# Ten instead of eight head pairs' score maxima in the expert phase, as full-array matmuls over zero-padded keys

## The reference

```python
xn = _layernorm(x)
# attention: a second layer norm, 16 heads of 8 features, softmax over 1024 keys
zn = (xn - mu) / jnp.sqrt(var + 1e-05) * ln_w + ln_b
q, k, v = split_heads(zn @ W_qkv + b_qkv)
attn = jax.nn.softmax(jnp.einsum('bhqd,bhkd->bhqk', q, k) / sqrt(8), axis=-1)
s = xn + concat_heads(attn @ v) @ W_proj + b_proj
# experts: all 8 are computed, the best 2 by the router count
h = gelu(xn @ W1[e] + b1[e])            # 128 -> 512
expert_out = h @ W2[e] + b2[e]          # 512 -> 128
g = silu(sum_e weights[:, e] * expert_out[e])
out = x + s * g
```

## Time and profile before

| | us |
|---|---|
| time, median of 3 runs (1129.79 to 1131.89) | 1130.94 |
| profiled execution, its time | 1131.14 |
| its span | 1129.3 |

### The profile page before, as it was taken

The page is one execution under the profiler, slowest core; times in us unless marked ns, Lnnn a source line. Parts: engine busy times, 40 slices in busy tenths (PEclk is TensorE's granted clock), DMA queues, the critical chain, the costliest instruction groups (busy, mean ns, idle before and its releaser), DMA issues.

```text
span 1129.3 us, 17260 instructions
## 1 busy us (share of the span) xinstructions
PE 1062.4 (94%) x6041; PEld 438.8 (39%) x6041; DVE 896.3 (79%) x1567; ACT 847.7 (75%) x1133; POOL 365.0 (32%) x534
## 2 busy tenths in 40 slices
PE   5698999999999999999999999999999999999995
PEld 4475656566666666663122222222121212212123
DVE  7566778777768687666999999999999999999715
ACT  6575666566666666667988898888889898988982
POOL 3795656656666666453010001000000000000001
PEclk9899999999999999998999999999999999999998
DMA  4523131414141322223111112111211111111102
GB/s 144 150 83 84 61 86 29 117 34 118 32 114 33 102 51 64 75 72 92 45 44 44 39 35 56 32 45 29 58 31 44 40 48 45 30 44 30 30 1 75
DMA packets 84992, 67.42 MB, mean 60 GB/s; under 512 B 9277, under 2 KB 71402, under 8 KB 84906
## 3 DMA queue, kind: packets, MB, share of 16 engines
q1 hardware_dynamic: 84906, 66.32, 21.7%
HBM read 51.08 MB, written 15.20 MB: 59 GB/s over the span
## 4 chain that ended last, share of the span: by engine, by line
PE 53%; ACT 19%; DVE 6%; issue 4%; ACTq 0%; DVEq 0%; POOL 0%; POOLq 0%
ACT p_ring L753 17%; PE psum L947 13%; PE psum L927 11%; PE psum L867 6%; PE psum L832 4%; PE psum L848 3%; PE psum L834 3%; PE psum L833 3%; PE psum L856 2%; PE psum L853 2%; PE psum L854 2%; DVE neg_max_half L1237 2%; PE psum L960 2%; DVE neg_max_half L1219 1%; PE psum L981 1%
## 5 line engine op out<-in xcount | busy, mean ns | idle before, releaser
L753 ACT ACTIVATE p_ring<-psum 128x1024 f32<-128x1024 f32 x512 | 500.7, 1023 | 66.0 <-PE psum L927 62.3
L1219 DVE TENSOR_REDUCE neg_max_half<-psum 128x1 f32<-128x512 f32 x768 | 486.3, 684 | 38.1 <-PE psum L867 29.0
L867 PE MATMUL psum<-k_max_stack,q_max_stack 48*128 48x512 bf16 x1024 | 300.6, 386 | 15.7 <-DVE neg_max_half L1237 9.6
L927 PE MATMUL psum<-q_stack,k_stack 51*128 51x512 bf16 x1024 | 279.1, 383 | 12.9 <-ACT p_ring L753 3.7
L947 PE MATMUL psum<-p_ring,v_sb 128*9 128x512 f32 x2048 | 268.5, 597 | 0.4 <-ACT o_sb L744 0.4
L716 ACT ACTIVATE h_hi<-psum,cols 128x512 fp32r<-128x512 f32 x192 | 132.0, 688 | 152.1 <-PE psum L834 147.9
L612 POOL TENSOR_TENSOR h_lo<-h_split,h_hi 128x512 fp32r<-128x512 f32 x128 | 164.5, 1289 | 141.0 <-ACT h_split L719 139.2
L1237 DVE TENSOR_REDUCE neg_max_half<-psum 128x2 f32<-128x1024 f32 x128 | 156.5, 1222 | 60.6 <-PE psum L867 60.4
L927 PEld LDWEIGHTS psum<-q_stack,k_stack 51*128 51x128 bf16 x1024 | 60.3, 94 | 305.8 <-ACT p_ring L753 281.4
L568 POOL CAST neg_max_parts<-neg_max_rest 128x16 bf16<-128x16 f32 x32 | 6.7, 211 | 510.6 <-DVE neg_max_rest L1228 510.6
L719 ACT ACTIVATE h_split<-psum,cols 128x512 f32<-128x512 f32 x192 | 130.9, 682 | 0.0
(11 more groups left out here) (114 smaller groups left out, 920.4 us busy)
## 6 DMA issues: line engine op xcount, KB each, us to landing
expert_w_bc<-expert_w_dram SPq DMA_DIRECT2D x64, 256.0 KB, 4.9
k_rows_dram<-qk_parts SPq DMA_DIRECT2D x24, 256.0 KB, 3.0
q_max_stack<-q_rows_dram SPq DMA_DIRECT2D x64, 96.0 KB, 2.5
k_max_stack<-k_rows_dram SPq DMA_DIRECT2D x64, 96.0 KB, 2.5
q_stack<-q_rows_dram SPq DMA_DIRECT2D x64, 96.0 KB, 2.5
k_stack<-k_rows_dram SPq DMA_DIRECT2D x64, 96.0 KB, 2.5
q_rows_dram<-qk_parts SPq DMA_DIRECT2D x8, 384.0 KB, 2.6
xz<-in_L_attn_z_dram SPq DMA_DIRECT2D x8, 256.0 KB, 3.2
```

The source lines that it names most:

```text
L753: act.activation(p_sb[:, n % PR, a, :, :].rearrange("p h t -> p (h t)"), scores_bank[s % 2], ACT.Exp, scale=SCALE).then_inc(S("P"), 1)
L867: return pe.matmul(to, q_m[rows, slot, t * P:(t + 1) * P], k_m[rows, slot, c * TG:(c + 1) * TG], start=True, stop=True)
L927: i = pe.matmul(scores_bank[s % 2][:, hh * TG:(hh + 1) * TG], k_s[rows, slot, kt * P:(kt + 1) * P], q_s[rows, slot, a * TG:(a + 1) * TG], ...
L1219: dve.tensor_reduce(mx[:, p % MXR, c, hh * NT + t:hh * NT + t + 1], ring_bank(("max", u)), AX.X, ALU.max, negate=True).then_inc(S("R"), 1)
```

## The change

- The first ten head pairs, not eight, have their maxima in the expert phase: 160 early units, in slots HT + 4 + (27 m) // 20, again from slot 36 to 250. 704 singles are left, over the same 240 blocks.
- k_m gets a second copy of its rows, one for each head: k_m[:, slot, 0, :] holds head 0's rows and zeros elsewhere, k_m[:, slot, 1, :] head 1's. An early unit is two matmuls with all 128 rows of q_m (both heads) as stationary operand and one of these as moving operand. The singles of the attention phase still use their 48 rows. Zeros are written once, k_m by VectorE and q_m by POOL at the start; SP's first row loads wait for both.
- w_t has no tile of its own and lies in xnT; ScalarE's copy into xnT therefore waits for the store of the group before.
- EARLY_TURN has ten entries: slots 60, 90, 122, 126, 154, 186, 190, 218, 233, 254 (before: 66, 92, 122, 154, 186, 218, 229, 257), and SP's lists of row loads and stores of maxima follow.

```diff
@@ -105,7 +105,7 @@
-        k_m = sb("k_max_stack", [P, 2, N], BF16)
+        k_m = sb("k_max_stack", [P, 2, 2, N], BF16)
@@ -145,7 +145,7 @@
-        wT = fs("w_t", [TT * E, P])
+        wT = xnT[0:TT * E, 0:P]
@@ -173,7 +173,7 @@
-        EARLY = 8 * 2 * NT
+        EARLY = 10 * 2 * NT
@@ -215,9 +215,10 @@
-        EARLY_AT = [HT + 4 + (27 * m) // 16 for m in range(EARLY)]
+        EARLY_AT = [HT + 4 + (27 * m) // 20 for m in range(EARLY)]
         EARLY_DONE = [EARLY_AT[(p + 1) * 2 * NT - 1] for p in range(EARLY_PAIRS)]
-        EARLY_TURN = [2 * HT + 2, 2 * HT + 28, 3 * HT + 26, 4 * HT + 26, 5 * HT + 26, 6 * HT + 26, 7 * HT + 5, 8 * HT + 1]
+        EARLY_TURN = [g * HT + at for g, at in ((1, 28), (2, 26), (3, 26), (3, 30), (4, 26), (5, 26), (5, 30), (6, 26),
+                                                (7, 9), (7, 30))]
@@ -384,7 +385,7 @@
-            sp.dma_start(dst.rearrange("t e p -> (t e) p"), wT[:, :]).then_inc(S("w_st"), 16)
+            sp.dma_start(dst.rearrange("t e p -> (t e) p"), wT).then_inc(S("w_st"), 16)
@@ -419,9 +420,11 @@
-                for t, to in ((q_dram, q_to), (k_dram, k_to)):
+                rows = slice(HALF * hh, HALF * hh + QROWS)
+                for t, to in ((q_dram, q_to[rows, slot, :]),
+                              (k_dram, k_to[rows, slot, hh, :] if k_to is k_m else k_to[rows, slot, :])):
                     rows_of = t[b].rearrange("(h d) s t -> h (d s) t", d=DH)[h]
-                    sp.dma_start(to[HALF * hh:HALF * hh + QROWS, slot, :], rows_of).then_inc(S(f"{name}{slot}"), 16)
+                    sp.dma_start(to, rows_of).then_inc(S(f"{name}{slot}"), 16)
@@ -485,22 +488,25 @@
+                    sp.wait_ge(S("q_zero"), 1)
+                    sp.wait_ge(S("k_zero"), 1)
...
-                if g in (2, 3):
-                    sp_max_rows(sp, g)
+                for p in {2: [2], 4: [5], 6: [8]}.get(g, []):
+                    sp_max_rows(sp, p)
...
-                if g > 2:
-                    sp_max_rows(sp, g + 1)
-                for p in ([], [], [0], [1], [2], [3], [4], [5, 6])[g]:
+                for p in {2: [3], 3: [4], 4: [6], 5: [7], 6: [9]}.get(g, []):
+                    sp_max_rows(sp, p)
+                for p in {2: [0], 3: [1], 4: [2, 3], 5: [4], 6: [5, 6], 7: [7, 8]}.get(g, []):
                     sp_store_max(sp, p)
+            sp_max_rows(sp, EARLY_PAIRS)
...
-            sp_store_max(sp, 7)
+            sp_store_max(sp, EARLY_PAIRS - 1)
@@ -623,6 +629,7 @@
+                pool.memset(q_m[:, :, :].bitcast(F32), 0.0).then_inc(S("q_zero"), 1)
@@ -664,6 +671,7 @@
+                    wait(act, "w_st", g, 16, 0)
@@ -697,7 +705,7 @@
-                    act.activation(wT[:, :], b5[0:TT * E, 0:P], ACT.Copy).then_inc(S("wT"), 1)
+                    act.activation(wT, b5[0:TT * E, 0:P], ACT.Copy).then_inc(S("wT"), 1)
@@ -860,13 +868,6 @@
-            def max_matmul(to, p, t, c, hh):
-
-                slot = p % 2
-                rows = slice(HALF * hh, HALF * hh + QROWS)
-                return pe.matmul(to, q_m[rows, slot, t * P:(t + 1) * P], k_m[rows, slot, c * TG:(c + 1) * TG],
-                                 start=True, stop=True)
-
@@ -875,7 +876,8 @@
-                    i = max_matmul(early_bank[:, hh, :], p, t, c, hh)
+                    i = pe.matmul(early_bank[:, hh, :], q_m[:, p % 2, t * P:(t + 1) * P],
+                                  k_m[:, p % 2, hh, c * TG:(c + 1) * TG], start=True, stop=True)
@@ -888,7 +890,9 @@
-                max_matmul(ring_bank(("max", u))[:, :], p, t, c, hh).then_inc(S("M"), 1)
+                rows = slice(HALF * hh, HALF * hh + QROWS)
+                pe.matmul(ring_bank(("max", u))[:, :], q_m[rows, p % 2, t * P:(t + 1) * P],
+                          k_m[rows, p % 2, hh, c * TG:(c + 1) * TG], start=True, stop=True).then_inc(S("M"), 1)
@@ -1247,6 +1251,7 @@
+            dve.memset(k_m[:, :, :, :].bitcast(F32), 0.0).then_inc(S("k_zero"), 1)
```

## The result

The changed kernel takes 1153.17 us (median of 4, 1152.62 to 1154.2) against 1130.37 in the same rounds: ratio 1.0197, 95% interval 1.0183 to 1.021. It is slower by 22.8 us; 14 were forecast, and the measured time lies inside the stated range.

A forecast was written before the change was run, and what follows sets the result against it. PE was taken to bound the expert phase, a PE-ScalarE loop with VectorE close behind the attention phase. Expert +32.5 us and attention -18.5 gave +14, 1145 us; own range 1135 to 1154, eight in ten 1124 to 1161.

The forecast's parts named there:

- Waits at slots 4j+2: Expert phase: 26 units following into 4j+2 wait 0.8 us each for a reduction queued behind VectorE's h_lo, 20.8 us.
- Waits into slots 4j+1 and 4j, and in slots with VectorE's layer norm, router and casts: Expert phase: 52 units at +0.1 each, 5.2 us; slots with VectorE's other work 8 us, between 0 and 20.
- PE's own work: Expert phase: 128 old pairs at 0.46 us for 0.52, -7.2; 32 new pairs at 0.46, +14.7.
- Attention: Attention phase: 64 fewer single maxima, head pair 17.6 us against 18.2, -18.5 us, from 8 to 39 us of gain.
- The rest: Span outside the early and attention maxima: forecast 0 us of change.
- The rule of the Trainium skill: Early max matmuls: row tiles up to twice the speed, so the full-array edit would lose 29 us instead of gaining 7.
- The faster rival: Whole kernel: stalls only take up waits due a slot later, and attention gives 22 to 25 us; -10 us, 1121; chance 0.21.
- The rival "slower by more": Expert phase: VectorE becomes the bound, +47 us there, less 18 in attention, 1160 us; chance 0.17.

The follow-up runs named there:

- half10: Changed kernel with its ten pairs and slots, but each early unit again as two matmuls in half arrays: 1152.37 us, ratio 1.0185.
- lowh: Changed kernel with VectorE's h_lo of slot 4j issued one slot later, behind the reduction of slot 4j+1's unit: 1135.61 us, ratio 1.0042.
- free2: Changed kernel with the same 160 early units, but the empty slot always a slot 4j+2: 1143.34 us, ratio 1.0111.
- spread10: Changed kernel with h_lo behind the reduction and eight free slots in every 32 put where VectorE has layer norm and router work: 1126.96 us, ratio 0.9964.
- spread8: Changed kernel with eight early pairs, full-array, h_lo behind the reduction, units in 19 chosen slots of 32, two transposes two slots later: 1125.24 us, ratio 0.9947.
- red_attn: Changed kernel with the attention phase's single maxima reduced over the first 256 of 512 keys only: 1146.82 us, ratio 1.014.
- red_early: Changed kernel with the early units' reductions over the first 256 of 512 keys only, matmuls unchanged: 1129.77 us, ratio 0.9987.
- full8: Changed kernel with eight early pairs and the old tables, units still full-array: 1130.78 us against 1130.84 for the kernel before, ratio 0.9994.
- spread8_half: spread8 with its early units as two matmuls in half arrays, as in the kernel before: 1130.17 us, ratio 0.9992.

## Why the prediction was right, and where its sizes were off

- **Direction and mechanism: right.** A head pair costs PE 16 x 0.45 = 7.2 us in the phase that PE bounds, and attention returned 15.0 us for two, so the trade is level before any wait; the waits decide it. half10 shows that the number carries the loss, lowh and free2 that it stands where it was said. The nearest to a comparison of the numbers alone, with few waits in both, is spread10 against spread8 (their tables of slots differ): early stretch 422.7 for 406.5, +16.2 (3.0 of it the clock's), attention 530.4 for 546.0, -15.6, time +1.7 us.
- **Waits at slots 4j+2: 20.8 us forecast, 22.1 measured** (26 places at 0.85). The step was read off one timeline.
- **Waits into slots 4j+1 and 4j, and in slots with VectorE's layer norm, router and casts: 5.2 + 8 us forecast, 17.4 measured.** These are most of the places left in lowh: units after slot 8 of a group waited up to 2.5 us. This term was mis-sized by 4 us, well inside the 0 to 20 stated.
- **PE's own work: +7.5 forecast, about +5** by the rows of the kernel after (0.45 for 0.46; half a us of the forecast is a slip, as 128 x 0.06 is 7.7 and not 7.2). Where hardly a unit waits the form gives 4.9 us in the time, not 7 to 9.
- **Attention: -18.5 forecast, -15.0.** The mechanism held: no block with four, the alternation stays. The plain block was right (2.11 on average). The block with the transposed output was mis-sized: 0.42 is its distance to a long block of 2.27, but the sum had added it to the mean of 2.11, and over that mean such blocks measured 0.53, which is 3.3 us in 30 head pairs. Transposes of maxima measured 0.43 for 0.4. red_attn shows that VectorE held nothing large any more.
- **The rest: 0 forecast, +2.0.** The first early reduction starts 1.1 us later (92.3 to 93.4). That isn't the change's work, as far as one execution tells: red_early has the same start-up code and its first reduction starts at 92.2. The other 0.9 us stay open.
- The three stretches missed by 3.0, 3.5 and 2.0 us, all to the same side, and so 14 became 22.5 in the span.
- **The rule of the Trainium skill.** By an estimate from the Trainium skill, "TensorEngine Tiling (Array Packing)", section "Theoretical Speedup", the full-array form should have lost 29 us. full8 measured no loss and spread8 against spread8_half a gain of 4.9, so here the measurement decides against it. What the section "Key Properties" of the same page of the Trainium skill says, that a change of the tiling mode drains the engine, fits the trace: the 0.33 us steps around half-array units are gone with the mode change.
- **The faster rival** wanted waits that are only moved. It was wrong for the changed kernel, where 40 us of waits were real, and right once they were small (spread8, spread8_half).
- **The rival "slower by more"** wanted VectorE's load as the bound and 1160 us. The time alone doesn't decide: 1153 lies as near to it as to 1145. free2, lowh and spread10 do: VectorE has the same work in all of them, and the time falls by 9.8, 17.6 and 26.2 us.

## What to carry to other kernels

Before work is moved into a phase that one engine bounds, write down both prices for a unit of it; here 7.2 us against 7.5 us, a level trade, so a gain had to come from somewhere else. What a denser schedule costs is then read from the queue of the partner engine: find the instruction that stands ahead of the one that is waited for, and move it first; one line of VectorE's order was worth 17.6 us. A free slot belongs where the partner engine has its other work, not at even distances (8.7 us from lowh to spread10). Once such waits are some 10 us of 1130, the next dependence can take most of what is removed: nothing of 6.6 us arrived in spread8, 1.3 of 10.9 in spread8_half.

## What was unexpected

Two row-tiled matmuls that run side by side cost PE 0.52 us between full-array ones, and the same product over padded zeros, as two matmuls one after the other, 0.45: the longer steps around a pair of 512 columns (0.33 for 0.23) cost more than its second matmul. Of these 0.07 us for each unit, 4.9 of 9 us reached the time, and 3.1 went into waits for reductions that start later.
